# A two-layer graph kernel: where the four shares of a step stand among the pairs of a matrix product

## The reference

```
def _ggc(x, adj, W, wih, whh, bih, bhh):
    m = adj @ (x @ W)
    gi = m @ wih.T + bih
    gh = x @ whh.T + bhh
    ...
    r = sigmoid(i_r + h_r); z = sigmoid(i_z + h_z); n = tanh(i_n + r * h_n)
    return (1.0 - z) * n + z * x
h = relu(_ggc(x, adj, W1, ...));  x = layernorm(x + relu(_ggc(h, adj, W2, ...)))

support = x @ weight
mask = (adj != 0)
rank = cumsum(mask, axis=1)
deg = rank[:, -1:]
k = minimum(deg, 100.0)
pos = rank - (deg - k)
w = mask * where(pos > 0, 0.5 ** (k - pos), 0.0)
x = layernorm(x + w @ support + bias)
```

## Time and profile before

| | us |
|---|---|
| median of three runs | 374.5 |
| profiled execution, its own time | 372.16 |
| its span | 370.4 |
| TensorE busy | 340.7 (92%) |
| VectorE busy | 294.7 (80%) |
| ScalarE busy | 173.8 (47%) |
| DMA, mean rate over the span | 314 GB/s |

### The profile page before, as it was taken

How to read it: one execution, slowest core, us unless ns; L and a number is a source line. 1 busy time by engine, 2 the same in 40 slices (tenths; PEclk the granted TensorE clock), 3 DMA queues, 4 the chain that set the end, 5 groups by cost and what they waited for, 6 DMA issues and landing times.

```text
span 370.4 us, 6473 instructions
## 1 busy us (share of the span) xinstructions
PE 340.7 (92%) x2414; PEld 155.7 (42%) x2422; DVE 294.7 (80%) x472; ACT 173.8 (47%) x206; POOL 23.9 (6%) x32
## 2 busy tenths in 40 slices
PE   4996979999999999999999989999898989899982
PEld 1431313333333333333333324444454544679982
DVE  1488978698896777879885569979696999798983
ACT  0003302013031220574593228674969696887992
POOL 1000000000000000000000010202020202002242
PEclk9999999999999999999999999999999999999998
DMA  7999999999999999999999999999999997100011
GB/s 226 407 402 377 408 379 409 368 410 396 373 408 365 401 304 378 375 361 336 313 362 364 357 381 408 355 387 280 399 334 408 319 406 251 30 3 4 2 58 59
DMA packets 36079, 116.34 MB, mean 314 GB/s; under 512 B 4176, under 2 KB 8528, under 8 KB 36048
## 3 DMA queue, kind: packets, MB, share of 16 engines
q1 hardware_dynamic: 36048, 115.92, 84.8%
HBM read 113.81 MB, written 1.05 MB: 310 GB/s over the span
## 4 chain that ended last, share of the span: by engine, by line
PE 55%; DMA 16%; ACT 11%; DVE 9%; issue 7%; POOL 1%; SPq 1%; POOLq 0%; ACTq 0%; DVEq 0%
PE m_acc L456 29%; DMA stream<-in_adj_t 13%; PE out L456 13%; ACT codes L721 4%; PE out L561 3%; DVE run L917 3%; DMA hx<-in_x_pairs 2%; PE rz_ps L534 2%; PE m_acc L561 2%; ACT wexp L721 2%; PE rz_ps L520 2%; PE rz_ps L513 1%; PE n_ps L513 1%; ACT stream L721 1%; PE n_ps L561 1%
## 5 line engine op out<-in xcount | busy, mean ns | idle before, releaser
L456 PE MATMUL m_acc<-stream,s_in 128*64 128x512 f32 x512 | 127.5, 608 | 8.4 <-DMA stream<-in_adj_t 6.0
L873 DVE TENSOR_SCALAR codes<-stream 128x1024 uint8<-128x1024 f32 x117 | 76.9, 686 | 14.5 <-DMA stream<-in_adj_t 14.5
L456 PE MATMUL out<-stream,s_mid 128*64 128x512 f32 x264 | 66.8, 595 | 2.1 <-DMA stream<-in_adj_t 1.8
L456 PEld LDWEIGHTS m_acc<-stream,s_in 128*64 128x64 f32 x512 | 32.9, 137 | 74.3 <-issue 48.3
L456 PE MATMUL m_acc<-stream,s_mid 128*64 128x512 f32 x248 | 57.0, 599 | 3.5 <-DMA stream<-in_adj_t 3.5
L814 POOL TENSOR_TENSOR rstd<-var,mhalf 128x4 f32<-128x4 f32 x16 | 22.0, 1377 | 342.9 <-DVE var L1027 342.9
L922 DVE SCALAR_TENSOR_TENSOR codes<-codes,run 128x1024 uint32<-128x1024 uint32 (+2 forms) x40 | 40.5, 1011 | 1.4
L917 DVE TENSOR_TENSOR run<-run,codes 128x2048 uint16<-128x2048 uint16 (+2 forms) x39 | 39.1, 1002 | 1.5
L721 ACT ACTIVATE wexp<-codes,code_bias 128x2048 uint16<-128x2048 uint8 x18 | 35.7, 1990 | 0.6 <-PE out L561 0.6
L456 PEld LDWEIGHTS out<-stream,s_mid 128*64 128x64 f32 x264 | 18.5, 137 | 39.3 <-issue 38.6
L456 PEld LDWEIGHTS m_acc<-stream,s_mid 128*64 128x64 f32 x248 | 16.4, 136 | 36.8 <-issue 34.9
(11 more groups left out here) (149 smaller groups left out, 404.1 us busy)
## 6 DMA issues: line engine op xcount, KB each, us to landing
stream<-in_adj_t SPq DMA_DIRECT2D x210, 512.0 KB, 6.6
hx<-in_x_pairs SPq DMA_DIRECT2D x8, 128.0 KB, 8.2
mx<-in_x_t SPq DMA_DIRECT2D x8, 128.0 KB, 6.8
mx<-hx SPq DMA_DIRECT2D x16, 64.0 KB, 5.3
x_res<-in_x_pairs SPq DMA_DIRECT2D x8, 128.0 KB, 5.0
out_nodes<-stream SPq DMA_DIRECT2D x8, 128.0 KB, 1.9
const<-in_consts SPq DMA_DIRECT2D x1, 358.0 KB, 7.8
bias_b<-in_bias SPq DMA_DIRECT2D x1, 128.0 KB, 7.9
```

What stands on the lines that cost most here:

```text
L456: last = nc.tensor.matmul(to[D * u:D * (u + 1), :], state[:, t * D:(t + 1) * D], stream[:, n % SLOTS, u * CW:(u + 1) * CW], start=start[u] ...
L873: nc.vector.tensor_scalar(edges(p // 2, b, 2 * (p % 2), 2), stream[:, n % SLOTS, :], 0.0, None, ALU.not_equal).then_inc(mask_made, 1)
```

## The change

One table is changed. Of the four shares of a step, two stood behind the gates (index 0) and two behind the node product (index 3). Now they stand at indices 0, 2, 5 and 8: behind the gates, behind the second, the fifth and the eighth pair. The tables of places, loads and expansions are as before.

```
-SHARE_AT = {t: (0, 0, 3, 3) for t in range(2, 7)}
+SHARE_AT = {t: (0, 2, 5, 8) for t in range(2, 7)}
```

## The result

| | before | changed |
|---|---|---|
| median of 19 runs each, us | 373.77 | 376.67 |
| ratio to before | | 1.0059, 95% interval 1.0040 to 1.0077 |
| profiled execution, span, us | 370.4 | 371.9 |

One run of the changed kernel, 379.81 us, lies more than 1.5% above the fastest and does not enter the ratio. The forecast was 375.9 us and no change that can be told (up to 0.5%, 376.4 us) with a chance of 0.62. The measured 376.67 is in the range and just beyond that line. The profiled execution of the changed kernel took 373.64 us, one of its shortest, so it cannot show all that the median has.

The account below looks back on a forecast made before the run. A ScalarE and VectorE loop was taken to bound the kernel from step 3's gates on, TensorE step 2. Switches 0.54 plus late place 0.91, 1.45 us on the median of 374.5, gave 375.9 us, range 373.5 to 377.6.

Parts of the forecast that it names:

- What bounds: From step 3's gates on, a loop of ScalarE and VectorE, every 17.79 us; step 2 is bound by TensorE.
- Item 1, the DMA waits: TensorE's three waits ahead of the last pair of steps 3 to 5, 3.2 us together, go; worth 0.
- Item 2, the switches: More changes between pairs and shares on TensorE cost 0.54 us in step 2, bounds 0.2 and 0.66.
- Item 3, the places: In step 6 ScalarE waits for a place freed late by a share; step 7's sigmoids 0.91 us later.
- Item 4, "I see nothing that absorbs it": Everything behind step 7's sigmoids is on the chain, so their delay reaches the end in full.
- The sum: Switches in step 2 plus the late place in step 6: 0.54 + 0.91 = 1.45 us.
- The clock, the rival with a chance of 0.02: Up to 3.0 us idle ahead of step 7's node product halves the clock, 5.3 us more: 381.3; chance 0.02.

Follow-up runs that it names:

- steps 3 to 5 alone: The kernel before with shares at indices 0, 2, 5 and 8 in steps 3, 4 and 5 only; ratio to before 1.0017.
- step 2 alone: The kernel before with shares at indices 0, 2, 5 and 8 in step 2 only; ratio to before 1.0026.
- step 6 alone: The kernel before with shares at indices 0, 2, 5 and 8 in step 6 only; ratio to before 1.0047.

## Why the prediction was right, and where it was not

- **What bounds.** Right, in the profiled execution. The loop of ScalarE and VectorE kept its 20.2, 17.8 and 17.8 us when TensorE's waits went.
- **Item 1, the DMA waits.** They went, for the reason given, and had no worth on the chain in the profiled execution; steps 3 to 5 alone are not faster (1.0017, 0.9995 to 1.0039). But "the worth of that on the end is 0" holds for short waits only (the profile of step 2 alone lost 0.8 us to one of 1.77), and what TensorE gained turned into idle time ahead of node 7, which has its own price.
- **Item 2, the switches.** 0.62 us measured against 0.54. The term that was mis-sized is the pair ahead of a share: two pairs take 230.53 - 228.66 = 1.87, so 0.96 for the last, which is +0.09 each and 0.27 for three, the upper bound, not 0.15. With it the sum is 0.66. The Trainium skill's rule (TensorE: Matmul & The Clock Gate, Step-by-step: what each phase is for) of weight loads that are pulled ahead does not show at this switch: the share's first load starts at 230.52, its matmul at 230.53.

```profile
230.52 0.90 PEld L561 LDWEIGHTS out<-sup,wexp 128*128 128x128 bf16 x16 [0.81 <-issue]
```

- **Item 3, the places.** The release came 313.35 - 305.53 = 7.82 us after the node, for 7.73 forecast; step 5 was covered, and step 2 was late by 0.5 us and hidden, for 0.6 forecast. The sigmoids of step 7 are later by 1.0 us (16.92 for 15.90), for 0.91.
- **Item 4, "I see nothing that absorbs it".** Wrong by 0.6 us. Two pieces of the code chain kept VectorE busy until 318.15, after the sigmoid that it needs (over at 317.4), so 0.6 of the 1.0 went into VectorE's slack and h_c of step 7 was later by 0.41 only. The chain of waits names the last releaser; it did not show that another engine was as late.
- **The sum.** 0.62 + 0.08 + 0.41 = 1.1 us by the profile, for 1.45. The seven runs at the upper clock values have 375.3 beside 373.75, 1.5 us, but these were not timed side by side.
- **The clock, the rival with a chance of 0.02.** This is the step that failed. The idle time was seen to grow (up to 3.0 us said, 2.22 measured), and the fall was dismissed because the clock had stood a wait of 1.56 us in one profile. (The row given for it ends at 320 us, inside the wait; the clock was 1.00 behind it too.) The kernel before had a low clock in 15 of 88 runs already. In the changed kernel it was 12 of 19; with 1.7 to 1.9 us between low and upper values in the two kernels that is (0.63 - 0.17) x 1.8 = 0.8 us, an estimate. With 1.1 to 1.5 for the schedule it makes 1.9 to 2.3, for 2.2 by the ratio. The price of one fall was over-sized: I had put half the clock on six shares, 5.3 us, and it lay on the node product and some two shares, 1.6.
- **Luck in the number.** The schedule was put 0.35 us too high by the profile and the clock at nothing, and these errors have opposite signs. The base was too high as well: 374.5 from three runs, where 19 runs gave 373.77. On that base the same sum gives 375.2 with an upper bound of 376.3, and the measured 376.67 lies beyond it; only the wider range holds it.

What stays open: why executions with the same idle time fall or not, and how much of step 6 alone (1.0047) is clock and how much is place. By the counts the clock is (0.58 - 0.17) x 1.7 = 0.7 of its 1.8 us, and without low clocks it still has 1.0033, but with an interval down to 1.0005.

## What to carry to other kernels

A short wait on a busy engine is worth nothing when another loop sets the period, and taking it away can cost: the idle time moves to the place where the engine must wait for that loop, and a longer gap there brings the clock down more often. Ask of each gap on TensorE how much it grows, not only whether it is on the chain, and look at the granted clock of every timed run, because one profile shows one draw of it. Where shares or other matmuls can stand in such a gap, put them there; in the kernel before it had no cost that can be told (0.9992), and it took back the change's loss (ratio 1.0068 to 1.0008). When a consumer is spread out, count which buffers are freed later, and by which in-order engine they are wanted.

## What the runs showed of the hardware

- In two profiles TensorE's granted clock fell from 2.4 to 1.2 GHz for 3.4 us behind 2.23 and 2.38 us of idle time, though the engine had had no longer pause since its first matmul; in three others it stayed up behind 2.22, 2.22 and 2.33 us. By the mean clock of the timed runs, 41 of 64 were low in the kernels with such a gap and 23 of 158 in those with 0.3 to 1.6 us. The same kernel does either from run to run.
- A change between fp32 pairs (128 x 64 weights) and bf16 shares (128 x 128) costs TensorE 0.09 to 0.10 us each way; the share's first weight load (230.52) begins with its matmul (230.53) and is not ahead of it.
